# Slot layer: the slots' inputs made with the normalised rows stationary and the dispatch weights streaming

## What is computed

```python
Xn = l2_normalize(X, axis=-1)                       # 625 x 768
logits = einsum('bmd,dnp->bmnp', Xn, sp)            # 625 x 32
D = softmax(logits, axis=1)                         # over the 625 nodes: dispatch
C = softmax(logits.reshape(b, m, n * p), axis=2)    # over the 32 slots: combine
X_tilde = einsum('bmd,bmnp->bnpd', Xn, D)           # 32 x 768: the slots' inputs
H = gelu(einsum('bnpd,ndh->bnph', X_tilde, W_down) + b_down)
Y_tilde = einsum('bnph,nhd->bnpd', H, W_up) + b_up
Y = einsum('bnpd,bmnp->bmd', Y_tilde, C)            # 625 x 768
```

## Time and profile before

| | |
|---|---|
| median of the timed runs | 1740.7 us |
| lowest and highest of the three | 1740.62 and 1742.16 us |
| profiled execution, span | 1740.0 us |
| what lies around its span | no time of its own is recorded beside the span; the runs' median is 0.7 us above it |
| TensorE busy with matmuls | 97% of the span |
| VectorE, ScalarE, GpSimd | 54%, 27%, 40% |
| mean granted TensorE clock | 0.988 |
| `f2_tilde` to the start of `f2_hidden` | 836.95 to 847.40 us |

### The profile page before, as it was taken

How to read it: one execution, slowest core, us unless ns; L and a number is a source line. 1 busy time by engine, 2 the same in 40 slices (tenths; PEclk the granted TensorE clock), 3 DMA queues, 4 the chain that set the end, 5 groups by cost and what they waited for, 6 DMA issues and landing times.

```text
span 1740.0 us, 25810 instructions
## 1 busy us (share of the span) xinstructions
PE 1682.7 (97%) x10227; PEld 1579.9 (91%) x10227; DVE 931.1 (54%) x1879; ACT 466.8 (27%) x875; POOL 690.3 (40%) x428
## 2 busy tenths in 40 slices
PE   8799999999999988899999999999999999999999
PEld 7699999997999988799377888989999999998999
DVE  8993537416866679857497554423112141225731
ACT  6443123203223138934222211101011011112310
POOL 1026865652445520060020175431644435342663
PEclk9899999999999999899899999999999999999999
DMA  2002222423212210014010022111221111110222
GB/s 90 1 28 70 73 69 65 142 78 128 64 55 64 64 56 10 1 47 143 7 43 1 11 85 64 57 45 37 73 64 55 46 51 59 55 55 30 64 73 72
DMA packets 42000, 99.84 MB, mean 57 GB/s; under 512 B 10509, under 2 KB 12143, under 8 KB 41895
## 3 DMA queue, kind: packets, MB, share of 16 engines
q1 hardware_dynamic: 37828, 87.87, 16.3%
q10 hardware_dynamic: 4066, 10.46, 1.7%
HBM read 96.39 MB, written 1.92 MB: 57 GB/s over the span
## 4 chain that ended last, share of the span: by engine, by line
PE 82%; DVE 11%; ACT 4%; issue 1%; POOL 1%; DVEq 0%; POOLq 0%; ACTq 0%
PE bank L2421 10%; PE bank L2423 10%; PE bank L2422 10%; PE banks L2421 9%; PE banks L2422 9%; PE banks L2423 9%; PE bank L2983 3%; PE banks L2983 3%; PE bank L3060 3%; PE bank L3065 3%; PE banks L3060 2%; PE banks L3065 2%; DVE tmp L1827 1%; DVE src_hot L1491 1%; PE banks L2835 1%
## 5 line engine op out<-in xcount | busy, mean ns | idle before, releaser
L833 POOL TENSOR_TENSOR w_hi<-raw,ones_r 128x768 fp32r<-128x768 f32 (+1 forms) x192 | 294.0, 1532 | 994.9 <-PE banks L2423 368.3
L836 POOL TENSOR_TENSOR w_lo<-raw,w_hi 128x768 fp32r<-128x768 f32 (+1 forms) x192 | 370.5, 1930 | 15.0
L2421 PE MATMUL bank<-w_hi,xT_hi 128*125 128x384 f32 (+2 forms) x560 | 187.8, 335 | 1.7 <-DVE small L1968 1.2
L2423 PE MATMUL bank<-w_hi,xT_lo 128*125 128x384 f32 (+2 forms) x560 | 186.7, 333 | 0.0
L2422 PE MATMUL bank<-w_lo,xT_hi 128*125 128x384 f32 (+2 forms) x560 | 186.5, 333 | 0.0
L2421 PE MATMUL banks<-w_hi,xT_hi 128*125 128x384 f32 (+2 forms) x440 | 151.8, 345 | 0.2 <-DVE xT_lo L1569 0.2
L2422 PE MATMUL banks<-w_lo,xT_hi 128*125 128x384 f32 (+2 forms) x440 | 151.4, 344 | 0.0
L2423 PE MATMUL banks<-w_hi,xT_lo 128*125 128x384 f32 (+2 forms) x440 | 151.3, 344 | 0.0
L1618 DVE TENSOR_TENSOR hT_lo<-tmp,hT_hi 128x312 fp32r<-128x312 f32 (+1 forms) x88 | 94.3, 1078 | 41.9 <-ACT hT_hi L970 41.5
L2421 PEld LDWEIGHTS bank<-w_hi,xT_hi 128*125 128x125 f32 x560 | 103.9, 186 | 5.0 <-DVE small L1968 1.4
L2422 PEld LDWEIGHTS bank<-w_lo,xT_hi 128*125 128x125 f32 x560 | 103.9, 185 | 2.5
(11 more groups left out here) (579 smaller groups left out, 3923.4 us busy)
## 6 DMA issues: line engine op xcount, KB each, us to landing
raw<-wa SPq DMA_DIRECT2D x92, 384.0 KB, 3.0
raw<-wc SPq DMA_DIRECT2D x76, 384.0 KB, 3.0
raw<-wb SPq DMA_DIRECT2D x28, 448.0 KB, 3.3
w_rows<-w_in ACTq DMA_DIRECT2D x1, 3072.0 KB, 12.6
bias<-bias_in ACTq DMA_DIRECT2D x6, 384.0 KB
w_first<-w_in ACTq DMA_DIRECT2D x1, 2304.0 KB, 11.2
w_down<-w_down_in SPq DMA_DIRECT2D x8, 288.0 KB, 5.2
w_up<-w_up_in SPq DMA_DIRECT2D x1, 2304.0 KB, 10.6
```

The source lines that it names most:

```text
L833: pool.tensor_tensor(w_hi[:, k, 0:width], raw[:, k, 0:width], ones[:, 0:1].to_broadcast([P, width]), ALU.mult).then_inc(S("unit_high"), 1)
L836: pool.tensor_tensor(w_lo[:, k, 0:width], raw[:, k, 0:width], f(w_hi[:, k, 0:width]), ALU.subtract).then_inc(S("unit_split"), 1)
L2421: tell_used(pe.matmul(dst, l_hi, r_hi, start=start, stop=False))
L2423: return pe.matmul(dst, l_lo, r_hi, start=False, stop=stop)
```

## The change

Steps 4 and 5 become one. For each of the six blocks k of the width and each tile n of nodes, `xn[:, n, block k]` (125 x 128) is stationary and `dispatch[:, n]` (125 x 32) streams. The result stands at once in the turned form, 128 x 192 in one bank, which VectorE copies to `tildeT`. `tilde`, its two multiplications and its six transposes go. The multiplication by `row_sum` moves behind W_down, into VectorE's two copies to `slot_hidden`.

```diff
-    several("f2_tilde", 2, "f2_tilde_read")
     several("f2_tildeT", 1, "f2_tildeT_read")
...
-            dve.wait_ge(*E("f2_row_total", 1))
-            for c in range(2):
-                await_group(dve, "f2_tilde", c)
-                TS(tilde[:, c * 384:(c + 1) * 384], bank("f2_tilde", c)[0:SLOTS, 0:384], row_sum[:], None, ALU.mult
-                   ).then_inc(S("f2_tilde_read"), 1)
             await_group(dve, "f2_tildeT", 0)
             dve.tensor_copy(tildeT[:].rearrange("p k s -> p (k s)"), bank("f2_tildeT", 0)[:, 0:KD * SLOTS]
                             ).then_inc(S("f2_tildeT_read"), 1)
...
+            dve.wait_ge(*E("f2_row_total", 1))
             for c in range(2):
                 await_group(dve, "f2_hidden", c)
-                dve.tensor_copy(slot_hidden[:, c * 384:(c + 1) * 384], bank("f2_hidden", c)[0:SLOTS, 0:384]
-                                ).then_inc(S("f2_hidden_read"), 1)
+                TS(slot_hidden[:, c * 384:(c + 1) * 384], bank("f2_hidden", c)[0:SLOTS, 0:384], row_sum[:], None, ALU.mult
+                   ).then_inc(S("f2_hidden_read"), 1)
...
             pe.wait_ge(*E("f2_dispatch_read", 1))
-            for c in range(2):
-                dst = open_bank("f2_tilde", c)
+            dst = open_bank("f2_tildeT", 0)
+            for k in range(KD):
                 for n in range(NT):
-                    last = pe.matmul(dst[0:SLOTS, 0:384], dispatch[:, n], xn[:, n, c * 384:(c + 1) * 384],
+                    last = pe.matmul(dst[:, k * SLOTS:(k + 1) * SLOTS], xn[:, n, k * P:(k + 1) * P], dispatch[:, n],
                                      start=n == 0, stop=n == NT - 1)
-                close(last, "f2_tilde", c)
+            close(last, "f2_tildeT", 0)
...
-            slots_turned("f2_tildeT", tilde, "f2_tilde_read")
```

More of the change, by code:

```diff
@@ L449, in families @@
                      ("f2_row_total", 1), ("f2_combine", 1), ("f2_dispatch_read", 1), ("f2_combineT_read", 2),
-                     ("f2_tilde_read", 2), ("f2_tildeT_read", 1), ("f2_hidden_read", 2), ("f2_hiddenT_read", 1),
+                     ("f2_tildeT_read", 1), ("f2_hidden_read", 2), ("f2_hiddenT_read", 1),
                      ("f2_masked", 1), ("f2_up_read", 2)):
@@ L683, in network @@
         combine_K = f2_new("combine_K", [3 * SLOTS, NP], f32r)
-        tilde, tildeT = f2_new("tilde", [SLOTS, D]), f2_new("tildeT", [P, KD, SLOTS])
+        tildeT = f2_new("tildeT", [P, KD, SLOTS])
         slot_hidden, hidden_T = f2_new("slot_hidden", [SLOTS, D]), f2_new("hidden_T", [P, KD, SLOTS])
```

## The result

The changed kernel's median is 1746.8 us over six runs (1745.79 to 1747.4), that of the kernel before 1741.46 us over six. The ratio is 1.0028, 95% interval 1.0018 to 1.0039: slower, by 3.1 to 6.8 us. The median lies 1.5 us above the forecast of 1745.3 and inside its range of 1738.5 to 1748.8; the likeliest case is the one that came.

What follows compares the result with a forecast made beforehand. It took TensorE, busy 97% of 1740.0 us, and the slot layer's chain as the bound. 3.17 + 2.26 + 0.06 - 0.85 = +4.6 us on 1740.7 gave 1745.3 us, 8-in-10 range 1738.5 to 1748.8.

Steps and rivals of the forecast that it cites:

- likeliest case: Slot layer: a load-bound stage at half clock throughout makes the kernel slower, 1745.3 us; chance 0.60.
- The stage, 1: Slots' inputs: sixty load-bound records at half clock, 0.216 us each, then tail, copy and hand-over; `f2_hidden` starts 3.17 us later.
- The half clock handed on, 2: `f2_hidden`: its 384-column stream now brings the clock back after 4.55 us at half, 2.26 us more.
- The multiplication, 3: Copies to `slot_hidden`: multiplying by `row_sum` takes 606 ns instead of 542, only the second on the path, +0.06 us.
- the cover: VectorE's one-hot tiles, 7.2 us, fit beside a stage of 7.8; were that gone, up to 0.6 us late.
- The later fall, 4: Between `f2_hidden` and `f2_up`: the half clock there, worth 1.7 us, may come or not; half counted, -0.85.
- The 0.7 us carried over from the profile: Whole kernel: the runs' median lies 0.7 us above the profiled 1740.0 us, giving the base of 1740.7.
- The clock coming back in the stage: Slots' inputs: loads back to back restore full clock, 1739.8 us, or 1737.6 with no fall ahead; chance 0.21.
- Quick loads: Slots' inputs: 128-column loads as quick as in transposes, sixty records at 0.124 us at half clock, 1740.2 us; chance 0.12.
- the one on the faster side: Slots' inputs: quick loads and the clock back, 1736.9 us, or 1734.6 with no half clock; chance 0.07.

Runs made afterwards that it cites:

- four_streamed: The changed kernel with each of the stage's thirty matmuls streaming its 32 dispatch columns four times (128 columns): median 1738.84 us, ratio to the kernel before 0.9983.
- scale_only: The kernel before with only the multiplication by `row_sum` moved to the copies to `slot_hidden`: median 1741.12 us, ratio to the kernel before 0.9990.
- warm_before: The kernel before with 13 unread 384-column matmuls in TensorE's three waits ahead of the combine's transposes: median 1739.85 us, ratio to the kernel before 0.9986.
- warm_twice: The changed kernel with 13 unread matmuls in the waits ahead and 64 columns streamed per matmul of the stage: median 1737.41 us, ratio to the kernel before 0.9971.
- warm_after: The changed kernel with 13 unread matmuls in the three waits ahead of the stage: median 1739.34 us, ratio to the kernel before 0.9979.
- warm_four: The changed kernel with 13 unread matmuls in the waits ahead and 128 columns streamed per matmul of the stage: median 1738.02 us, ratio to the kernel before 0.9978.
- twice_streamed: The changed kernel with each of the stage's thirty matmuls streaming its 32 dispatch columns twice (64 columns): median 1746.13 us, ratio to the kernel before 1.0020.

## Why the prediction was right, step by step

**The stage, 1.** Forecast 12.96 us plus the hand-over, `f2_hidden` 3.17 us later after the stage's start than before. Measured: 838.20 to 851.55 is 13.35 us where it was 10.45, so +2.9. The step from load-bound rows was right; the price of a record was 0.211, the lower of the two bounds, not 0.216. That the clock stays at half for the whole stage was the assumption on which the forecast stood, chosen against the earlier trace rows; it held, and `four_streamed` shows why both readings had something: with 32 columns behind each load the clock did not come back in 12.7 us, with 128 it came back, as it did in the earlier trace rows with 129. One reading was weaker than it looked: at 0.322 us for 384 columns the 129 of the earlier trace rows stream for 0.108 us, as long as their distance of 0.106, so these rows alone don't tell loads from streaming. The 0.211 of the new stage, with a quarter of the columns, bears the price out.

**The half clock handed on, 2.** Forecast +2.26 us in `f2_hidden`; measured 10.30 against 7.91, +2.39, with the clock back 4.8 us after its start instead of 4.55.

**The multiplication, 3.** 605 ns for the one on the path against 542: as forecast, and `scale_only` bears it out. VectorE's one-hot tiles were done before the first read was due (VectorE stood idle 2.9 us for the first half of `f2_hidden`): the cover held.

**The later fall, 4.** Weighed at one half, -0.85; in the profiled execution it is gone and saves 9.56 - 7.87 = 1.69. This is the term that was mis-sized, by 0.84, and it was a guess between two outcomes. That it can go either way is shown: it is in `warm_before`, `four_streamed` and `warm_twice`, not in `warm_after` and `warm_four`.

The sum inside the layer is thus 2.9 + 2.39 + 0.06 - 1.69 = 3.7 us, against 4.6 forecast; the medians differ by 5.3 and the ratio says 3.1 to 6.8. The 1.25 us that the profiled executions differ by ahead of the layer were in no step, and the profile of `four_streamed` shows that one program can differ by as much from one execution to the next. What makes the medians differ by 1.7 us more than the layer is open; the six runs of the kernel before alone spread over 2.2 us. So it is in part luck that the total came as near as it did: the sum is 0.9 us too large for the layer and 0.7 too small for the medians. The other 0.8 of the 1.5 us is the base, 1740.7 from three runs, where six have 1741.46. The 0.7 us carried over from the profile was no constant either: the runs that have their own span on record last 1.7 to 1.9 us longer than it.

**The rivals.** The clock coming back in the stage: it didn't, in the change; it did in `four_streamed`. Quick loads: a load at full clock takes 0.19 us in `warm_after`, not 0.14, and sixty take 6.7 us in `warm_four`, so this rival and the one on the faster side are out for these matmuls, 128 columns of plain fp32. (The rival's own time was added up wrongly: 2.4 us earlier, 2.3 and 0.06 later and 0.85 for the later fall make 1739.8, not 1740.2. Nothing else rests on it.)

The loads of `warm_after` (ns min/median/max):

```profile
L2928 PEld LDWEIGHTS banks<-dispatch,xn x60: 190/192/338, 836.5 to 843.9; 125*128 125x128 f32 x60
```

The Trainium skill (TensorE: Matmul & The Clock Gate, Weight-path perf modes) has no fast load for fp32, and by this row the trace agrees for these matmuls; the fp32 transposes of the earlier trace rows load in 0.140 us all the same. The Trainium skill (the same page, LDWEIGHTS (loading the stationary operand)) has the number of columns over 1.2 ns for a load, an estimate of 107 ns for 128. At full clock the loads of this case stand 0.111 us apart, so the distance agrees, though a load by itself is recorded with 0.19; at half clock they stand 0.211 apart, which the formula does not say, and the measurement decides.

## What to carry to other kernels

Swapping which operand stands still trades streaming for loads, and it should be priced twice: the loads at the pace of a load-bound row (here 0.11 us for 128 columns against 0.03 for the streaming behind it), and the clock that such a stage gets or loses, which here was worth more than everything the change removed (0.8 us at full clock, against 2.4 lost in `f2_hidden` alone). A stage without a gap on TensorE is not safe from the half clock, as this one shows: what it streams has to be looked at, and the stage behind it pays until the clock is back. If a short chain of small stages must wait on other engines, unread matmuls in those waits can be worth their place: thirteen of them made the kernel before 0.7 to 4.2 us faster and the changed one 8 to 9.

## What was not expected of the hardware

Streaming the same 32 columns four times instead of once made the kernel 8 us faster (0.9983 against 1.0028). With 32 columns behind each load of 128 the clock fell 5.5 us into a stage that left TensorE no gap (`warm_after`); with 64 it did not fall in `warm_twice` but, once down, did not come back in the 12.8 us of `twice_streamed`; with 128 it came back after 1.8 us (`four_streamed`). Each of these is read from one profiled execution; the runs' times bear out the second half, 64 columns against 128 from half clock, in every run.
